# Moving the summation one-hots of two transformer layers from VectorE to ScalarE, with added GpSimd waits in four gather and scatter loops

## The reference, cut to what matters

```python
def transformer_conv(x, edge_index, Wq, bq, Wk, bk, Wv, bv, Ws, bs):
    q, k, v = (x @ Wq + bq), (x @ Wk + bk), (x @ Wv + bv)     # 4 heads of 32
    alpha = einsum('ehc,ehc->eh', q[dst], k[src]) / sqrt(32)
    ealpha = exp(alpha - segment_max(alpha, dst)[dst])
    attn = ealpha / segment_sum(ealpha, dst)[dst]
    return segment_sum(attn * v[src], dst) + x @ Ws + bs
h = relu(transformer_conv(x, ...1))
out = transformer_conv(h, ...2)
```

## Time and profile before

| | us |
|---|---|
| median of 3 runs (3877.59 to 3880.7) | 3878.28 |
| profiled execution, its own time | 3893.77 |
| its span in the trace | 3892.1 |
| busy: PE 76%, DVE 64%, POOL 62%, PEld 51%, ACT 27% | of the span |
| mean granted TensorE clock | 0.829 |
| POOL gathers of the two transformer layers, 832 | 839.3 busy |
| DVE one-hots for the sums, L2009, 208 | 143.3 busy |

### The profile page before, as it was taken

How to read it: one execution, slowest core, us unless ns; L and a number is a source line. 1 busy time by engine, 2 the same in 40 slices (tenths; PEclk the granted TensorE clock), 3 DMA queues, 4 the chain that set the end, 5 groups by cost and what they waited for, 6 DMA issues and landing times. The chain is left out here.

```text
span 3892.1 us, 57650 instructions
## 1 busy us (share of the span) xinstructions
PE 2947.8 (76%) x14303; PEld 2002.8 (51%) x14345; DVE 2492.3 (64%) x8135; ACT 1048.7 (27%) x2557; POOL 2423.7 (62%) x2427
## 2 busy tenths in 40 slices
PE   6987997746666567999977999766677776676773
PEld 3455895534444433444435777643465564364663
DVE  8886553251111377999988888873567775384876
ACT  3730664110000043333315666620011120010211
POOL 2747777647777347777754666117777734777770
PEclk8975557568888788999988999888798898888986
DMA  2222222322222147888851222026787755687872
GB/s 70 68 60 52 62 62 58 48 61 53 53 53 53 29 90 197 239 236 236 241 138 57 68 70 70 22 78 181 196 243 223 226 167 139 182 245 194 252 238 65
DMA packets 397387, 493.91 MB, mean 127 GB/s; under 512 B 64035, under 2 KB 293992, under 8 KB 397138
## 3 DMA queue, kind: packets, MB, share of 16 engines
q0 software_dynamic: 92160, 244.83, 24.3%
q1 hardware_dynamic: 304978, 245.98, 21.8%
HBM read 376.23 MB, written 114.36 MB: 126 GB/s over the span
## 5 line engine op out<-in xcount | busy, mean ns | idle before, releaser
L1918 POOL DMA_INDIRECT got<-kv_table,pair_src x832 | 839.3, 1009 | 495.4 <-issue 249.3
L686 POOL DMA_INDIRECT y_got<-y_table,y_idx x416 | 399.7, 961 | 166.2 <-issue 126.4
L1164 POOL DMA_INDIRECT got<-t_table,tile_src x392 | 378.3, 965 | 175.4 <-issue 118.8
L2167 PE MATMUL psum<-acc 125*128 x1664 | 285.1, 324 | 219.0 <-DVE h L1984 195.1
L1313 PE MATMUL sums<-msg,hot 128*125 128x260 f32 x1664 | 394.0, 390 | 31.3 <-POOL msg L1255 28.6
L2167 PEld LDWEIGHTS psum<-acc 125*128 125x128 f32 x1664 | 243.7, 224 | 297.1 <-issue 295.8
L2179 PE MATMUL psum<-h,acc 128*128 128x128 f32 x1664 | 324.0, 329 | 68.1 <-ACT hot_b L2142 37.3
L1313 PEld LDWEIGHTS sums<-msg,hot 128*125 128x125 f32 x1664 | 305.9, 189 | 119.1 <-issue 72.3
L1984 DVE TENSOR_TENSOR h<-psum,got 128x512 f32<-128x512 f32 x208 | 143.4, 690 | 348.1 <-DMA got<-kv_table,pair_src 315.1
L1255 POOL TENSOR_TENSOR msg<-rows,msg 128x512 f32<-128x512 f32 x208 | 246.3, 1204 | 188.1 <-DVE msg L1281 148.7
L628 PE MATMUL psum<-zeros 128*128 128x512 bf16 (+1 forms) x946 | 340.6, 490 | 3.5 <-issue 2.4
(11 more groups left out here) (506 smaller groups left out, 5705.3 us busy)
## 6 DMA issues: line engine op xcount, KB each, us to landing
v_rows<-got SPq DMA_DIRECT2D x208, 256.0 KB, 3.4
small<-v_rows SPq DMA_DIRECT2D x208, 256.0 KB, 4.8
dst_row<-dst_rows SPq DMA_DIRECT2D x312, 128.0 KB, 4.8
rows<-x_rows SPq DMA_DIRECT2D x104, 256.0 KB
x_rows<-small SPq DMA_DIRECT2D x104, 128.0 KB, 3.6
x_rows<-got_w SPq DMA_DIRECT2D x104, 128.0 KB, 4.5
got<-kv_table,pair_src POOLq DMA_INDIRECT x832, 3.8
y_table<-y_stage SPq DMA_DIRECT2D x25, 448.0 KB
```

What stands on the lines that cost most here:

```text
L686: pool.indirect_dma_start(out=got[:, slot, j, :], out_offset=None, in_=y_table[:, :], in_offset=bass.IndirectOffsetOnAxis(ap=m.y_idx[:, co ...
L1164: pool.indirect_dma_start(out=got[:, col % ring, :], out_offset=None, in_=table[:, :], in_offset=bass.IndirectOffsetOnAxis(ap=m.tile_src[: ...
L1918: pool.indirect_dma_start(out=got[:, slot, j, :], out_offset=None, in_=kv_table[:, :], in_offset=bass.IndirectOffsetOnAxis(ap=m.pair_src[: ...
L2167: last = t.matmul(work[:, j * P:(j + 1) * P], hot_t[:, g % 2, j // 2, j % 2, :], m.acc[:, bass.ds(ws[j], 1), 0:D].rearrange("q o d -> q (o ...
```

## The change

In conv_layer, ScalarE makes the lane one-hot of groups 0 to 87 (early is 88, the first group of the last chunk) in both forms by itself: four absolute differences |iota - lane's row| into a new tile away, a wait on its own result, then max(0, 1 - away) once into hot (float32) and once into hot_b (bfloat16). VectorE makes it for the last 16 groups only. TensorE's add also waits for hot_made. The tile away lies in windows 8 and 9 of the keys and values, so ScalarE first waits until these are stored. GpSimd gets a further wait in four loops.

```diff
@@ sort_edges, GpSimd
             for t in range(BY_DMA):
+                if 6 * t // 5 > 8:
+                    pool.wait_ge(placed, 6 * t // 5 - 8)
                 pool.indirect_dma_start(out=code_table[:, :], ...
@@ relation_layer, GpSimd
                 if g >= SL:
                     pool.wait_ge(used, g - SL + 1)
+                elif g > 2:
+                    pool.wait_ge(counted, min(4 * g - 8, groups))
@@ gat_scores, GpSimd
                 if g >= slots:
                     pool.wait_ge(turned, g - slots + 1)
                     pool.wait_ge(scored, (g - slots) // 2 + 1)
+                    pool.wait_ge(z_done, 4 * (g - 3))
                     pool.wait_ge(aside[slot], 32 * (g // slots))
@@ conv_layer
+        away = m.acc_all[:, 8:10, D:3 * D].rearrange("l w (j q) -> l w j q", j=2)
+        away_ready, hot_made, early = sem("away_ready"), sem("hot_made"), CHUNK_AT[last_chunk] // G
@@ GpSimd
                 slot = g % 8
+                if g >= 7:
+                    pool.wait_ge(q_done, g - 6)
                 if g >= 8:
                     pool.wait_ge(used, g - 7)
@@ VectorE, messages
                 if s >= 2:
                     dve.wait_ge(summed, s - 1)
-                v.tensor_tensor(hot[:, s % 2],
+                if s >= early:
+                    v.tensor_tensor(hot[:, s % 2],
@@ ScalarE
+            def make(s):
+                if s >= 2:
+                    act.wait_ge(summed, s - 1)
+                if s:
+                    act.wait_ge(hot_kept, s)
+                for k in range(G):
+                    last = nc.scalar.activation(away[:, k // 2, k % 2, :], m.iota[:, 0:P], ACT.Abs, scale=-1.0,
+                                                bias=m.pair_row[:, s * G + k:s * G + k + 1])
+                last.then_inc(away_ready, 1)
+                act.wait_ge(away_ready, s + 1)
+                nc.scalar.activation(hot[:, s % 2], away, ACT.Relu, scale=-1.0, bias=m.iota[:, 1:2]).then_inc(hot_made, 1)
+                nc.scalar.activation(hot_b[:, s % 2], away, ACT.Relu, scale=-1.0, bias=m.iota[:, 1:2]).then_inc(hot_kept, 1)
+
             def keep(s):
-                act.wait_ge(hot_ready, s + 1)
+                act.wait_ge(hot_ready, s - early + 1)
@@
+            act.wait_ge(kv_stored, 32 * (W // 5))
             for c in range(len(CHUNK)):
                 weigh(c)
                 if c < last_chunk:
                     for s in groups_of(c):
-                        keep(s)
+                        make(s)
@@ TensorE, add
                 pe.wait_ge(msg_ready, s + 1)
+                pe.wait_ge(hot_made, min(s + 1, early))
                 pe.wait_ge(hot_kept, s + 1)
```

## The result

| | median us | runs |
|---|---|---|
| before | 3879.45 | 4, 3877.59 to 3880.7 |
| changed | 3908.6 | 4, 3902.57 to 3914.54 |

The changed kernel is slower by 29 us: the ratio is 1.0076, with a 95% interval of 1.0062 to 1.009. The profiled execution took 3910.89 us (span 3909.1), 17 more than the profiled one of before, which was itself 14 above its own median. On a third chip, which the last four experiments use, two executions far above all others (one of 17 of the kernel before, 6852.77 us, and one of six of E9, 13657.24 us) stay out of the ratios.

The account below looks back on a forecast made before the run. GpSimd's unbroken gather issue was taken to bound the transformer layers. Transformers -2.6 and gat_scores +3 gave +0.4 on the profiled 3893.8 us, or 3879 on the median 3878.3; eight in ten needed 3860 to 3912.

Parts of the forecast that it names:

- the third rival: ScalarE's group takes 3.0 us, or gat_scores stalls each round, some 0.3 on each of 98 groups; 3900 to 3914, chance 0.14.
- The wait of gat_scores: GpSimd's new wait for z four groups back in gat_scores: holds ordinarily, stalls at low clock; +3 us, between 0 and +8.
- 1.1 us before the gather starts; it is close, and it holds: In gat_scores, z ordinarily ends at 1595.6, ahead of the gather at 1596.72, so the new wait does not delay it.
- The one-hots: Moving one-hots to ScalarE in the transformers: chunks 1 and 2 gain, chunk 3 loses; one layer -1.3 us, both -2.6.
- ScalarE's group: ScalarE's time for one group's one-hots: 2.69 us, bounds 2.6 and 3.0, making it slowest in the stretches with sums.
- Chunk 1, -4: Layer 1, chunk 1: sums last 90.3 instead of 77.8 us, the lag is made up, shorter gathers gain 4 us.
- I take 60%: Share of the gathers' lengthening beside the sums that goes; bounds none and all of some 18 us a layer.
- Chunk 2, -3.5: Layer 1, chunk 2: sums 90.3, last add and query 2.5, six steps 13.1; 105.9 us instead of 109.4.
- Chunk 3, +6.2: Layer 1, chunk 3: 75.6 us instead of 69.4, as only four groups without sums are left to absorb slower ones.
- The first rival: Transformer gathers keep the lead and run freer: -12 us a layer, 3858 in all; chance 0.25 with partial forms.
- The clock rival: TensorE's clock falls in the sums while it waits for ScalarE: +19 us a layer, 3917; chance 0.15.
- The other three waits at 0: GpSimd's new waits in sort_edges, the relational layer and the transformers are satisfied in time and cost 0.

Follow-up runs that it names:

- E9: The changed kernel with the gat_scores wait one group looser and chunk 3's one-hots on VectorE; 4642.54 us against 4872.76 for before, on the third chip.
- E2: The kernel before with the new wait of gat_scores alone; 3892.98 us, ratio 1.0038.
- E6: The kernel before with the wait of gat_scores one group looser than in the change (g - 4); 3880.55 us, ratio 1.0.
- E10: The kernel before with the wait of gat_scores one group tighter than in the change (g - 2); 4973.18 us, ratio 1.0194, on the third chip.
- E3: The changed kernel without any of its four new GpSimd waits, so the one-hots on ScalarE alone; 3894.66 us, ratio 1.0035.
- E8: The kernel before with VectorE's one-hots of groups 2 to 87 left out, the sums using old ones; 3869.77 us, ratio 0.9971.
- E4: As E3, but ScalarE makes groups 0 to 63 only and chunk 3 stays on VectorE; 3875.64 us, ratio 0.9988.
- E1: The changed kernel without the new wait of gat_scores; 3895.36 us against 3880.09 for before, ratio 1.004.
- E11: As E3, but ScalarE leaves out the fourth difference of each group after the first; 4873.0 us, ratio 0.9997, on the third chip.
- E7: The changed kernel with no new waits, ScalarE making odd groups' one-hots below 88 and VectorE the even ones'; 3879.78 us, ratio 1.0.

## Why the prediction was right in its range and wrong in its terms

The forecast, 3879 and no change, is 29.6 us low. The time of 3908.6 lies within the 3860 to 3912 given for eight cases in ten, by 3.4 us, and at a time of the third rival (3900 to 3914, chance 0.14). Both are luck. That rival wanted a ScalarE group of 3.0 us or a stall of gat_scores in each round, and neither came; two other losses add up to its time. Two terms of the sum failed, by about 10 and 17 us.

**The wait of gat_scores: +3 forecast, within 0 to +8; +13 to +14.7 measured.** The step that failed is "1.1 us before the gather starts; it is close, and it holds". It goes wrong twice. First, it lets the gather start the moment z ends. In the changed kernel and in E2 no gather that follows the wait starts less than 0.84 us after the end of its z, and nearly every held one starts at 0.84 or 0.85 (1592.82 to 1593.67 above). So 0.27 of the 1.1 us were left. In the trace of the kernel before, 41 of the 98 gathers start less than 0.84 us after that z, and these are the ones that the new wait touches. Second, I read one ordinary group and took its margin for all. The loop shows what the margin is, by E2's medians: group k's four gathers take 4.7 us; from the end of the last to the first turning of that group pass 4.6 us (4.05 to 5.85 over the groups); from there to the end of z of group k - 1 another 4.75; then 0.84 to the next gather. That is some 14.9 us, and the wait g - 3 allows three groups of 5.0, 15.0. The margin is about 0.1 us, and the landing varies by far more, so one group in four or five is held for over 0.05 us beyond the usual (20 of 98 in E2, 22 in the changed kernel). With g - 4 there are 5 us more, and E6 costs nothing; with g - 2 there are 5 fewer, and E10 waits in every other group. The long single pause which I did price did come, 3.40 at 1919.03 against my 3.2, but it was a small part. The third rival said "gat_scores stalls each round", 0.3 on each group; in its place come pauses mostly of 0.4 to 1.2 on each fourth or fifth.

Of the 13, some 6 are the pauses of 1.86 before gathers 113, 209, 305 and 401. They come in kernels in which GpSimd is held by waits. What they are stays open: packets of the instruction queues stand near some of them (1614.4 in E2, just before the gather at 1614.49) and near none at gather 209.

**The one-hots: -2.6 forecast, +15 measured** (E3; +10.7 between the two first traces). By chunks and in the mean of both layers:

| | forecast | changed kernel |
|---|---|---|
| chunk 1 | -4 | -1.4 |
| chunk 2 | -3.5 | -0.2 |
| chunk 3 | +6.2 | +7.7 |

- *ScalarE's group*: 2.69 forecast, 2.74 measured. This was right, and so were the stretches of about 90, 90 and 69 us (91.0, 89.2, 67.6), ScalarE's share (92, 92 and 90%) and its taking over as the slowest engine.
- *Chunk 1, -4*: the failing step is "I take 60%" of 6.5. The mean gather beside the sums did fall, from 1.065 to 70.28/69 = 1.019; that takes 40% of the lengthening of each, not 60 (0.114 to 0.068). And the sums now last 91 us instead of 78, so 69 gathers lie beside them instead of 57: 0.068 x 69 = 4.7 us of lengthening are left of 6.5. That is a gain of 1.8, near the 1.2 of the trace. I guessed the share and took it from the old count. E8 shows the ceiling: with the one-hots of these groups gone entirely the gathers lose 12.1 us in two layers and the kernel 10.9, where I had put "all of the 18" a layer as the upper bound.

  Against the median gather of 0.947, 39.3 us of lengthening are left over the 832 gathers in E8, of 51.4. Taken gather by gather, the trace of before shows what lengthens them. The 241 gathers with a one-hot or a message running on VectorE in their first 0.947 us take 1.114 us in the mean, the other 591 take 0.966; the 241 hold 40 of the 51.4 us. The DMA engines' load, which is also higher in the sums (0.90 against 0.68 in chunk 0), is not it: gathers without such a neighbour take 0.963 where that load is over 0.95 (84 of them) and 0.967 where it is lower. In E8 197 gathers still have such a neighbour, mostly a message, and take 1.090. Half of the instructions are gone, but four fifths of the touched gathers stay, each almost as long. This is why leaving out half of the instructions does not take half of the lengthening. The Trainium skill (SBUF — State Buffer, "SBUF: two separate sides") ascribes such waits to VectorE instructions with two SBUF inputs. The trace agrees in which gathers are long; the amount does not follow the number of instructions.
- *Chunk 2, -3.5*: the failing steps are the sums' 90.3 and "the last add and query 2.5", by 1 us each. The last one-hot was made at 3058.22, 91.3 us after the start, and the score step behind the last add and query came at 3061.71, 3.5 later: 94.8 in all for my 92.8. The remaining six steps took 13.3 (forecast 13.1). In layer 2 the last one-hot came at 93.8. The wait for the next gather, at which before spent its last steps (4 to 5 us each from 3048.44 on), is gone in exchange.
- *Chunk 3, +6.2*: the mechanism was right, and the size low by 1.5: after the sums come 9.9 us instead of 6.9, and in layer 1 the sums were 1.1 shorter than forecast. E4 removes the loss by leaving this chunk on VectorE, which shows where it stood.

The two chunks which should have paid for the third gave 1.6 us instead of 7.5. One trace against another is loose for such amounts: over the runs of the first two chips in which a chunk's code is the same, its length varies by up to 3 us.

**The first rival**, gathers running freer, fell with E8: even without any price the move is worth 11 us, not 24. **The clock rival** fell too: 0.88, 0.88 and 0.83 in the sums, with low stretches at the start of a chunk as before. 0.83 in chunk 3 is under the 0.85 that I named as a sign; in E3, with the same one-hots, it is 0.89 and the chunk is still 75.8 us long, so the clock did not make most of it. **The Trainium skill's rule** (ScalarE: Activation LUTs, "Rules for kernel authors") that simple elementwise work belongs on VectorE held in chunk 3 (2.74 us a group there against 0.60) and was near neutral in chunks 1 and 2 (E4).

**The other three waits at 0**: right on the first two chips, as E1 and E3 agree within 0.7 us. On the third chip this step would have been wrong by over 160 us in the other direction: I priced a wait by what it delays, and never asked what GpSimd's unbroken issue does to the others.

The two mended forms are E4 (3875.64, faster by 4.5) and E9, faster by 230 on the third chip. E9 did not run on the first two, nor the changed kernel on the third; by E1, E3, E4 and E6 E9 should stand near E4 on the first two, which is an estimate.

## What to carry to other kernels

A wait on a counter a fixed number of groups back closes a loop: add up its whole round, with the time from the counter's rise to the next start and the spread of a transfer's landing, over many groups and compare it with that number of groups' time; if the margin is smaller than the spread, allow one group more. Before work is moved off an engine, ask what leaving it out altogether would bring (E8: 11 us); that is the ceiling, and a slower engine costs in full wherever a short stage has no slack to absorb it. Back-to-back issue by GpSimd can be harmless on one chip and stall the rest on another, so a wait which costs nothing may be worth keeping.

## What the runs showed of the hardware that I had not expected

- The same kernel takes 3880 us on two chips and 4873 on a third, with a gather as long on all (L686: 945 ns in the median before, 947 in E11). Why was not tried. In E11 the whole kernel moves 101 GB/s in the mean, against 126 in the changed kernel.
- On the third chip, while GpSimd issues its scatters without a pause, TensorE, VectorE and ScalarE get one round done in 10 to 11 us, and 1 GB/s is moved in place of 60. One wait on TensorE's counter in that loop lifts it (E9). What is held back was not tried. The stores of y_table alone are an unlikely cause: the code makes them once in seven rounds, and the stop comes in each.
- GpSimd, once held by waits, pauses some 1 to 2 us at every 96th gather of gat_scores (1.77 to 1.86 in E2, 0.95 to 1.86 in the changed kernel, 1.86 in E10, 1.86 to 2.15 in E11, which has no added wait but in which GpSimd is held in every other group); in E1, E3, E4, E6 and E7 the same places show 0.6 us or less.
- A gather held by a wait on TensorE's counter starts 0.84 us after the profile's end of the matmul that releases it (E2, the changed kernel, E10 on the third chip).
- Which gathers of the transformers are long goes with VectorE's instruction beside them and not with the DMA load (before: 1.114 us beside a one-hot or message, 0.963 with none beside and the DMA engines over 95% busy).
